# A new slot table for the projection and finish work that runs beside a ScalarE-bound attention loop

## The reference

```python
q_h = exp_map_at_origin(q_t, c); k_h = ...; v_h = ...     # q_t = split_heads(layernorm(x) @ W_q.T)
diff_norm_sq = xnsb - 2.0 * xy + ynsb
denom = jnp.maximum((1.0 - c * xnsb) * (1.0 - c * ynsb), EPS)
arg = jnp.maximum(1.0 + 2.0 * c * diff_norm_sq / denom, 1.0 + EPS)
dist = 1.0 / sqrt_c * jnp.arccosh(arg)
weights = jax.nn.softmax(-beta_pos * dist - attention_bias, axis=-1)
out_tan = jnp.einsum('bhst,bhtd->bhsd', weights, v_tan)
x = x + out_heads_tan @ W_o.T
x = x + fp8_gemm(layernorm(x), kernel) + bias
```

## Time and profile before

| | us |
|---|---|
| median of 3 runs | 1992.56 |
| lowest, highest | 1990.39, 1993.75 |
| profiled execution, its run | 1994.49 |
| profiled execution, its span | 1992.7 |
| ScalarE busy (share of the span) | 1869.9 (94%) |
| TensorE busy | 1788.6 (90%) |
| VectorE busy | 1142.9 (57%) |

### The profile page before, as it was taken

The page is one execution under the profiler, slowest core; times in us unless marked ns, Lnnn a source line. Parts: engine busy times, 40 slices in busy tenths (PEclk is TensorE's granted clock), DMA queues, the critical chain, the costliest instruction groups (busy, mean ns, idle before and its releaser), DMA issues.

```text
span 1992.7 us, 29554 instructions
## 1 busy us (share of the span) xinstructions
PE 1788.6 (90%) x10713; PEld 603.1 (30%) x10713; DVE 1142.9 (57%) x2825; ACT 1869.9 (94%) x1094; POOL 12.8 (1%) x35
## 2 busy tenths in 40 slices
...
GB/s 56 112 49 144 54 54 103 42 134 43 112 44 78 77 44 112 43 101 75 23 134 22 110 67 44 112 43 134 40 107 52 56 90 43 123 43 53 33 33 23
DMA packets 112953, 142.54 MB, mean 72 GB/s; under 512 B 35691, under 2 KB 61548, under 8 KB 112748
## 3 DMA queue, kind: packets, MB, share of 16 engines
...
## 4 chain that ended last, share of the span: by engine, by line
ACT 54%; PE 24%; issue 14%; DVE 4%; ACTq 3%; DMA 0%; DVEq 0%; SPq 0%
ACT U L1217 28%; ACT U L1224 26%; PE ps L1100 8%; PE ps L401 6%; PE ps L1115 5%; ACTq L1265 2%; PE ps L695 2%; DVE U L1294 1%; PE ps L1138 1%; PE ps L406 1%; PE ps L1142 1%; DVE U L1285 1%; DVE rows L554 0%; DMA U<-in_L_attn_W_o_dram 0%; ACT e L529 0%
## 5 line engine op out<-in xcount | busy, mean ns | idle before, releaser
L1224 ACT ACTIVATE U<-U 128x2048 f32<-128x2048 f32 x512 | 997.1, 1949 | 0.3
L1217 ACT ACTIVATE U<-ps 128x2048 f32<-128x2048 f32 x500 | 955.7, 1911 | 35.5 <-PE ps L1100 31.6
L1100 PE MATMUL ps<-q_T,k_T 18*128 18x512 f32 x4096 | 632.5, 652 | 133.0 <-ACT U L1217 107.7
L1115 PE MATMUL ps<-U,vals 128*32 128x512 f32 x4096 | 560.4, 620 | 29.4 <-ACT U L1224 28.9
L1100 PEld LDWEIGHTS ps<-q_T,k_T 18*128 18x128 f32 x4096 | 195.9, 187 | 356.8 <-ACT U L1217 296.4
L401 PE MATMUL ps<-wT,xnT 128*128 128x384 f32 x512 | 232.0, 545 | 4.9 <-DVEq L1318 2.5
L490 DVE COPY qkv<-ps 128x384 f32<-128x384 f32 x112 | 62.4, 557 | 243.7 <-PE ps L401 243.6
L1115 PEld LDWEIGHTS ps<-U,vals 128*32 128x32 f32 x4096 | 81.7, 109 | 205.4 <-ACT U L1224 159.2
L401 PEld LDWEIGHTS ps<-wT,xnT 128*128 128x128 f32 x512 | 81.1, 194 | 197.0 <-issue 132.4
L1138 PE MATMUL ps<-woT,ident 128*128 128x256 f32 x340 | 121.8, 441 | 3.8 <-DVEq L1318 3.6
L406 PE MATMUL ps<-ident,rows 128*128 128x128 f32 x512 | 107.2, 308 | 4.9 <-DVE rows L554 2.4
...
## 6 DMA issues: line engine op xcount, KB each, us to landing
...
```

Of the source, the lines that this page charges most:

```text
L1100: ins = pe.matmul(g.ps[:, 2 * pair + i, :], a.k_T[HB * h:HB * h + RD, b % 2, hg, kt * P:(kt + 1) * P], a.q_T[HB * h:HB * h + RD, G % 3, hg ...
L1115: ins = pe.matmul(g.ps[HB * h:HB * h + VW, 6, :], a.vals[:, b % 2, kt, (hg * HPG + h) // 2, DH * (h % 2):DH * (h % 2) + VW], U[:, n % RING ...
L1217: act.activation(U[:, n % RING].rearrange("p b n -> p (b n)"), chunk(n), ACT.Ln, scale=-2.0 / EPS, bias=1.0).then_inc(freed, 1)
L1224: act.activation(U[:, n % RING], U[:, n % RING], ACT.Exp, scale=exponent).then_inc(exp_done, 1)
```

## The change

The slots of the side work get other numbers, and three pieces of VectorE's work move with them.

- The products M0 to M7 go from slots 7, 8, 9, 10, 12, 13, 15, 16 to 5, 7, 8, 10, 11, 13, 15, 16. X0 and X1 go into the two halves of slot 4. R0 to R7 get slots 25 to 29 and 31 to 33, one each. A0 goes from slot 27 to the second half of slot 30, A1 from slot 31 to the second half of slot 34. Group 2 (`SECOND_USES`) keeps its R and A slots and has M3 in slot 9.
- `BARE` becomes steps 5, 8 and 16 (before: 7).
- VectorE: the squares go from slots 9, 11, 14, 17 to 9, 12, 13, 16. The three Newton steps go to slots 17, 18 and 19 (before: one in 18, two in 19). `vals` goes from slot 20 to slot 35. The queries' rows are scaled in slot 23, the keys' in 24 (before both in 24, keys first). Pieces of the finish go from slots 8, 28, 32 to 7, 27, 33.
- ScalarE: `e` goes from slot 21 to slot 20.
- SyncE: the stores of a group go from slot 34 to 36, the result's store from 33 to 34.
- Group 14's finish starts at step 18 of group 15 (before: 23).

```diff
-BARE = 7
-SHORT_SLOTS = {23: (23, 24), 24: (25, 26), 25: (27, 28), 26: (29,), 27: (30, 31), 28: (32,), 29: (33,), 30: (), 31: ()}
+BARE = (5, 8, 16)
+SHORT_SLOTS = {18: (18, 21), 19: (19, 22), 20: (20, 23), 21: (24,), 22: (25,), 23: (26,), 24: (27,), 25: (28,),
+               26: (29,), 27: (30, 31, 32), 28: (33,), 29: (34,), 30: (), 31: ()}
...
-        if k == 21:
+        if k == 20:
             act.wait_ge(n_rdy, n + 1)
             act.activation(e[:, :, :], nrm[:, :, :], ACT.Exp, scale=g.M2SC).then_inc(e_rdy, 1)
...
-        if k == 18:
+        if k == 17:
             root_guess(v, step, ss[:, :, :], y[:, :, :])
             newton(v, step, ss[:, :, :], y[:, :, :], y2[:, :, :], 1)
+        if k == 18:
+            newton(v, step, ss[:, :, :], y[:, :, :], y2[:, :, :], 1)
         if k == 19:
-            newton(v, step, ss[:, :, :], y[:, :, :], y2[:, :, :], 2)
+            newton(v, step, ss[:, :, :], y[:, :, :], y2[:, :, :], 1)
             v.tensor_tensor(nrm[:, :, :], ssqk, yqk, ALU.mult).then_inc(n_rdy, 1)
-        if k == 20:
+        if k == (31 if n == 2 else 35):
...
+            if n >= 2:
+                scale_rows(v, n, (0,))
         if k == 24:
-            scale_rows(v, n, (1, 0))
+            scale_rows(v, n, (1,))
...
-                    unused = n > 2 and s != BARE and not in_step(G, s, 0) + in_step(G, s, 1)
+                    unused = n > 2 and s not in BARE and not in_step(G, s, 0) + in_step(G, s, 1)
```

More of the change, by code:

```diff
@@ L49 @@
 EARLY = 4
-PROJECT_SLOTS = 35
-FINISH_SLOTS = 34
-PROJECT_USES = {("X", 0): (4, BOTH), ("X", 1): (5, BOTH),
-                ("M", 0): (7, BOTH), ("M", 1): (8, BOTH), ("M", 2): (9, BOTH), ("M", 3): (10, BOTH),
-                ("M", 4): (12, BOTH), ("M", 5): (13, BOTH), ("M", 6): (15, BOTH), ("M", 7): (16, BOTH),
-                ("R", 0): (25, BOTH), ("R", 1): (26, BOTH), ("R", 2): (27, 0), ("A", 0): (27, 1),
-                ("R", 3): (28, BOTH), ("R", 4): (29, BOTH), ("R", 5): (31, 0), ("A", 1): (31, 1),
-                ("R", 6): (32, BOTH), ("R", 7): (33, BOTH)}
+PROJECT_SLOTS = 37
+FINISH_SLOTS = 35
+PROJECT_USES = {("X", 0): (4, 0), ("X", 1): (4, 1),
+                ("M", 0): (5, BOTH), ("M", 1): (7, BOTH), ("M", 2): (8, BOTH), ("M", 3): (10, BOTH),
+                ("M", 4): (11, BOTH), ("M", 5): (13, BOTH), ("M", 6): (15, BOTH), ("M", 7): (16, BOTH),
+                ("R", 0): (25, BOTH), ("R", 1): (26, BOTH), ("R", 2): (27, BOTH), ("R", 3): (28, BOTH),
+                ("R", 4): (29, BOTH), ("A", 0): (30, 1), ("R", 5): (31, BOTH), ("R", 6): (32, BOTH),
+                ("R", 7): (33, BOTH), ("A", 1): (34, 1)}
 TOLD = 12
@@ L366, in sync @@
             sp.dma_start(xt[:, :, :], g.x_g[n + 1]).then_inc(x_in, 16)
-        if k == 34:
+        if k == 36:
             b, u = n // 2, n % 2
@@ L538, in first_vector @@
         step(v.tensor_scalar(ss[:, :, :], ss[:, :, :], EPS * EPS, None, ALU.max))
-        vector(v, n, 18, step)
-        vector(v, n, 19, step)
-        if n == 0:
-            v.wait_ge(zeroed, ZEROED)
-        vector(v, n, 20, step)
+        for k in (17, 18, 19, 35):
+            if k == 35 and n == 0:
+                v.wait_ge(zeroed, ZEROED)
+            vector(v, n, k, step)
         vector(v, n, 21, step)
@@ L582, in vector @@
             ins.then_inc(xn_rdy, 1)
-        if k in (9, 11, 14, 17):
-            t = {9: 0, 11: 1, 14: 2, 17: 3}[k]
+        if k in (9, 12, 13, 16):
+            t = {9: 0, 12: 1, 13: 2, 16: 3}[k]
             v.wait_ge(a.b7_copied, uses.after(("M", n, 2 * t + 1)))
@@ L590, in vector @@
                 step(v.tensor_scalar(ss[:, :, :], ss[:, :, :], EPS * EPS, None, ALU.max))
-        if k == 18:
+        if k == 17:
             root_guess(v, step, ss[:, :, :], y[:, :, :])
             newton(v, step, ss[:, :, :], y[:, :, :], y2[:, :, :], 1)
+        if k == 18:
+            newton(v, step, ss[:, :, :], y[:, :, :], y2[:, :, :], 1)
         if k == 19:
-            newton(v, step, ss[:, :, :], y[:, :, :], y2[:, :, :], 2)
+            newton(v, step, ss[:, :, :], y[:, :, :], y2[:, :, :], 1)
             v.tensor_tensor(nrm[:, :, :], ssqk, yqk, ALU.mult).then_inc(n_rdy, 1)
-        if k == 20:
+        if k == (31 if n == 2 else 35):
+            step = first or Steps(v, g_steps, 2 * (n - 2))
             step(v.tensor_scalar(vg[:, :, :], y[:, :, 2 * H:], g.ZS, 1.0, ALU.mult, ALU.min))
@@ L629, in vector @@
             v.tensor_reduce(amax[:, :], a4[:, :, :].rearrange("p t h -> p h t"), AX.X, ALU.max).then_inc(amax_rdy, 1)
+            if n >= 2:
+                scale_rows(v, n, (0,))
         if k == 24:
-            scale_rows(v, n, (1, 0))
-        assert first or step.n == OWN.get(k, 0), (k, step.n)
+            scale_rows(v, n, (1,))
+        assert first or k in (31, 35) or step.n == OWN.get(k, 0), (k, step.n)
     p = Shared()
```

37 lines of the change are left out of this document (19 added, 18 removed).

## The result

The changed kernel took 2035.65 us (median of 6 runs, 2031.92 to 2044.11). The kernel before, run beside it, took 1991.47 us (1984.75 to 1993.85). The ratio is 1.0233, with a 95% interval of 1.0204 to 1.0262: the change made the kernel 2.3% slower. The prediction was 2056 us with a range of 2010 to 2088.

A forecast was written before the change was run, and what follows sets the result against it. ScalarE, busy for 94% of the span, was taken as the bound. The terms -7.2 + 14.7 + 39 + 20 + 5 - 3.7 - 1.8 - 1.5 gave +64.5 us, 2057 us; forecast 2056 us, range 2010 to 2088.

The forecast's parts named there:

- Part 2: Step 16: `e` waits 1.4 us for `nrm`, a net 1.13 us in each of 13 groups, +14.7 us.
- Part 3: Behind step 16: TensorE idles 2.35 us and its clock falls, 3.0 us in each of 13 groups, +39 us.
- Rival A: Behind step 16: TensorE keeps its clock, so only the stalls remain, +25.5 us or 2018 us; chance 0.14.
- Part 4: Steps 30 to 1: A1, Y0 and X1 make the distances late, mean 1.55 us in 13 groups, +20 us.
- (e): Step 1: the finish's last piece now stands ahead of step 2's S copy, delaying M1: +0.4 a group, +5 us.
- (b): Group seam: VectorE's work on A1 delays Y0's copy, then Y1's distances: +0.1 us in even or +0.6 in odd groups.
- (a): Group seam: A1 waits for Q0's copy and the distances run only after it, making Ln late: +0.3 us.
- (c): Group seam: `vals` runs between the copies of Y1 and X0, so X1 is late: +0.7 us.
- Part 1: Steps 5 to 7: spacing the products removes 0.55 us in each of 13 groups, -7.2 us.
- Part 5: Group 0: M3's wait goes, -6 us, but X1 and M0 at half clock cost +2.3; net -3.7 us.
- Part 6: Last group: the fall near 1931 us goes, -4.4, and half a fall in bare steps adds +2.6; net -1.8 us.
- Part 7: The rest: VectorE loses row scaling and A0 in group 8's open unit, -1.5 us; R turns, squares and stores 0.

The follow-up runs named there:

- the kernel with the filler: The changed kernel with the filler products put back in step 16 (bare steps 5 and 8 alone), `e` still in slot 20: 2018.25 us, ratio 1.0138.
- the experiment's: The kernel before with group 2's products alone in new slots (X1 beside X0, M0 to M4; R7 in 12): 1987.24 us against 1988.34, ratio 0.9986.
- the fastest kernel: The changed kernel with `e` back in slot 21 and A0 and A1 back in slots 27 and 31: 1973.34 us, ratio 0.9933.

## Why the prediction was right, and where it wasn't

The sign, the order of the costs and their places were right. The time lies inside the range and 20 us below the forecast.

**Part 2, `e`.** Right, in mechanism and in size. I had worked out a wait of 1.4 us and a net loss of 1.13 a group, 14.7 us in all. Counted from the moment at which `e` could have begun, the wait is 1.36 us, and steps 16 and 17 together lost 14.7. That the last half us agrees is luck: without most of the falls, in the kernel with the filler, these steps lose 14.2. The single chain of the earlier trace rows gave this, since every link of it was in the trace before. Putting `e` back took it away.

**Part 3, the clock.** The mechanism was right and its size too large. TensorE's idle time is 2.34 us (forecast 2.35), and the clock fell in 11 of 13 groups (I had said 8 to 13). The term that failed is the 3.0 us a group. I had it from falls of 7 and 10 us that cost 3.8 and 4.0; here seven of eleven lasted 3.4 us and cost 1.6 each (1.85 less the 0.26 of a group without a fall), four lasted 6.8 us and cost 3 or slightly more. That gives 25.5 us in step 18, and 27.1 with a later fall in group 9, against 39. The two groups without a fall account for 6 us of the difference and the price of a fall for 9; against them stand the 2 us of step 18 that aren't the clock's, and 1.6 in group 9. This is 12 of the 23 us by which the sum missed. Rival A, the stalls without the clock, is what the filler in step 16 comes near to: 2018.25 us measured, 2018 worked out. That they meet is partly luck, since three falls are left in that kernel and the terms of the products and the seam were off in opposite directions.

The rows that I set against each other for part 3, falls behind 1.72 and 2.09 us and none behind 0.89, weren't the whole record. The fall of the earlier trace rows followed two shorter spells of TensorE, in a bare step:

```profile
1854.03 1.07 PE L1115 MATMUL ps<-U,vals 128*32 128x512 f32 x8 [0.56 <-ACT U L1224]
...
1855.80 1.81 PE L1100 MATMUL ps<-q_T,k_T 18*128 18x512 f32 x8 [0.70 <-ACT U L1217]
```

So the length of the last spell by itself didn't tell whether a fall would come. The Trainium skill (TensorE: Matmul & The Clock Gate, Why this matters for your kernels) would have kept the clock through the gap of 2.34 us in step 16; by 11 of 13 groups the trace disagrees with it.

**Part 4 and (e), the seam.** Forecast +25 us, measured +19.7, from partly different causes. (b) was right in its mechanism: A1's pieces push Y0's copy, and 0.79 in even and 0.33 in odd groups is what A1 alone does in the kernel before, for the 0.6 and 0.1 forecast. (a) was over-priced: 0.12 us, and 0.05 in the changed kernel, for 0.3. The two errors nearly cancel. (c), X1 behind `vals` for 0.7, was taken as an independent term, and it is none: `vals` alone costs 0.03 us a group (0.35 us over groups 1 to 13 between the two kernels with A0 and A1 back), A1 alone 0.02 in steps 1 and 2, both together 0.57 a group. They are in series on VectorE, and what A1 leaves of the slack decides the price of `vals`. Nor was (e) a term of its own: the finish's last piece and Y0 to X0 use the same slack, and with A1 back nothing of it is left but 0.3 us in step 2. What I missed is A0. I had it among the moves that cost nothing; in slot 30 it stands in step 26 behind the normalisation, and takes 0.28 us a group, 3.7 us.

**Part 1, products.** -7.2 was too much. Steps 6 and 7 gave 4.6 us back. The first 0.15 of the 0.55, in step 5, doesn't go, and where the packed step 4 and 5 stand now another 0.1 us appears. Alone, the spacing is worth 0.23 us in a plain group, and 1.0 us over groups 1 to 13.

**Part 5, group 0.** -3.7 was forecast, -6.5 seen in the changed kernel's trace, -3.9 in the experiment's, with a scatter of 3 us in that group when nothing is changed there. The term that failed for the changed kernel is the +2.3 for X1 and M0 at half clock: steps 5 and 6 took 2.3 us less there, not more. The stretch of half clock from 64 us on lasted 20 us before and 10 us in the changed kernel, and why it ended sooner isn't shown. In the experiment's trace it lasted 20 us, and the two steps took 1.4 us more.

**Part 6, the last group.** -1.8 was forecast, -7.6 measured in groups 14 and 15. The term of -4.4 for the finish was exact. What failed is the price of the bare steps: I had left the old fall of the earlier trace rows standing and added half a fall (+2.6). In the changed kernel one fall came in their steps, behind the same two spells of 0.56 and 0.70 us, and it was short (windows view):

```profile
1910.70:1914.10 3.40, 3.40 (x15) 0.70 (x10) 0.00 (x0) 3.40 (x3) 0.00 (x0) 0.50 0.00 0
```

It cost 1.2 us, where the old one, 10.2 us long, had cost 4.1 in steps 8 to 10. In two kernels that change nothing there no fall came in these steps at all (group 15's excess 8.2 us with A1 moved and 8.3 with the products spaced, 15.0 before). So that part, 2.9 us, can't be booked as a gain of the change. In those two the finish's stall was only 1.0 us, with no fall behind it, so the 4.4 holds where the clock falls in it.

**Part 7, the rest.** The steps of the open units took 0.2 us (group 5) and 0.3 us (group 8) less, against -1.5 forecast for group 8 alone.

**What stays open.** Why two groups of thirteen keep the clock over the same idle spell, and why falls last 3.4 or 6.8 us, isn't settled. It isn't the group: groups 3 and 7 kept it in the changed kernel, and 2, 7 and 12 with `vals` back in slot 20, over the same 2.34 us. Part of the difference between kernels of this study in groups 0, 14 and 15 is where such falls happen to lie: the fastest kernel has one of 10.2 us in group 14 (an excess of 4.1 us for 1.0), behind spells of 0.56 and 0.70 us in the bare step 8.
